# Experts one at a time with their weights as the moving operand, and a last stage in which ScalarE applies mean and deviation

## The reference

```
# mixture of experts, E = 64, rows gathered to 128 slots per expert
h  = silu(einsum('ecd,eid->eci', xb, w1)) * einsum('ecd,eid->eci', xb, w3)   # I = 176
yb = einsum('eci,edi->ecd', h, w2)                                           # D = 256
y  = zeros.at[tok].add(yb * weight)            # scattered back, added up
# second attention, after linear attention over 16 heads of 16
out = einsum('bhnd,bhde->bhne', qrh, kv) * z[..., None]
res = out + x
return (res - mean(res)) / sqrt(var(res) + 1e-12) * gamma + beta
# end of the model
x = x + s * silu(y + z)       # s: the attention's result
```

## Time and profile before

| | |
|---|---|
| median of 3 runs | 5537.14 us |
| the profiled execution | 5540.01 us, of which its span 5538.4 us |
| experts: first gather to last scatter | 5079.85 to 5310.77 us |
| last stage: from its first instructions to the end | 5316.9 to 5538.4 us |
| PE, DVE, ACT, POOL busy over the span | 89%, 75%, 54%, 53% |

### The profile page before, as it was taken

The page is one execution under the profiler, slowest core; times in us unless marked ns, Lnnn a source line. Parts: engine busy times, 40 slices in busy tenths (PEclk is TensorE's granted clock), DMA queues, the critical chain, the costliest instruction groups (busy, mean ns, idle before and its releaser), DMA issues. The chain is left out here.

```text
span 5538.4 us, 79645 instructions
## 1 busy us (share of the span) xinstructions
PE 4910.3 (89%) x26068; PEld 2909.0 (53%) x26068; DVE 4156.5 (75%) x8613; ACT 3011.0 (54%) x6489; POOL 2936.8 (53%) x1617
## 2 busy tenths in 40 slices
PE   6788888888885699999999999999999999998886
PEld 2233233233322477776555566666665555665765
DVE  3999999999999699999433477777763337995259
ACT  4877886887776477777211255555541114453232
POOL 4999999999999465655111244444431110002732
PEclk9898888889887799999999999999999999999997
DMA  5666566566555223223112111111111133444768
GB/s 134 152 157 148 142 160 159 139 150 160 147 132 129 77 85 91 86 88 103 46 57 63 45 35 35 37 38 36 46 52 47 57 117 129 159 141 126 196 147 177
DMA packets 493021, 585.39 MB, mean 106 GB/s; under 512 B 59446, under 2 KB 372548, under 8 KB 488516
## 3 DMA queue, kind: packets, MB, share of 16 engines
q1 hardware_dynamic: 461412, 554.19, 36.7%
q0 software_dynamic: 29184, 18.78, 2.3%
q10 hardware_dynamic: 2016, 7.34, 0.4%
HBM read 416.67 MB, written 180.37 MB: 108 GB/s over the span
## 5 line engine op out<-in xcount | busy, mean ns | idle before, releaser
L684 POOL TENSOR_TENSOR db<-durep,brep 128x2048 f32<-128x2048 f32 x256 | 1160.5, 4533 | 101.4 <-DVE p_h L589 87.6
L536 ACT ACTIVATE p_h<-dlrep,am 128x512 f32<-128x512 f32 x1024 | 700.4, 690 | 159.8 <-DVE hh L600 134.4
L589 DVE TENSOR_TENSOR_SCAN p_h<-p_h,hlast,db 128x512 f32<-128x512 f32 x576 | 718.3, 1278 | 21.8 <-ACT hlast L525 17.7
L1302 POOL TENSOR_TENSOR rot_cos<-rot_cos,rot_sin 128x1024 f32<-128x1024 f32 x128 | 302.2, 2361 | 536.1 <-DVE rot_sin L1223 536.1
L1298 POOL TENSOR_TENSOR rn<-n,mhalf 128x16 f32<-128x16 f32 x128 | 374.7, 2928 | 266.7 <-DVE n L1233 266.6
L600 DVE TENSOR_TENSOR hh<-p_h,crep 128x512 f32<-128x512 f32 x768 | 516.1, 672 | 0.0
L352 PE MATMUL p_acc<-hh,fold 128*32 128x512 f32 x2048 | 310.1, 681 | 207.4 <-DVE hh L600 206.1
L1665 POOL TENSOR_TENSOR grstd<-grstd,mhalf 128x4 f32<-128x4 f32 x32 | 32.6, 1019 | 729.1 <-DVE grstd L1582 728.9
L980 PE MATMUL p_s<-qkT 64*128 64x128 f32 x4096 | 300.3, 286 | 75.6 <-DVE nb L1188 74.4
L1567 ACT ACTIVATE gg<-p_s,b 128x512 f32<-128x512 f32 x160 | 110.0, 687 | 448.5 <-PE p_o L1510 265.8
L1091 ACT ACTIVATE probB<-probB,nb 128x256 f32<-128x256 f32 x512 | 254.4, 499 | 164.9 <-DVE nb L1188 164.9
(11 more groups left out here) (290 smaller groups left out, 11730.1 us busy)
## 6 DMA issues: line engine op xcount, KB each, us to landing
dlrep<-delta_rows SPq DMA_DIRECT2D x256, 256.0 KB
durep<-drive_rows SPq DMA_DIRECT2D x256, 256.0 KB
ew<-in_L_ffn_w SPq DMA_DIRECT2D x192, 176.0 KB
first_queries_keys<-qs SPq DMA_DIRECT2D x128, 256.0 KB, 2.4
qk<-first_queries_keys SPq DMA_DIRECT2D x64, 512.0 KB, 3.8
brep<-bc_rows SPq DMA_DIRECT2D x64, 256.0 KB
crep<-bc_rows SPq DMA_DIRECT2D x64, 256.0 KB
delta_rows<-dl SPq DMA_DIRECT2D x64, 256.0 KB
```

Of the source, the lines that this page charges most:

```text
L536: act.activation(p_h[:, (i % BANKS) * CH:(i % BANKS + 1) * CH], dlrep[use % 2][:, j], ACT.Exp, scale=am[:, q, j, g:g + 1]).then_inc(s_ex, 1)
L589: dve.tensor_tensor_scan(out=state, data0=bank, data1=db[s % 2][:, j], initial=0.0 if first else hlast[:, i % TILES:i % TILES + 1], op0=AL ...
L684: pool.tensor_tensor(out=db[s % 2][:], in0=durep[use % 2][:], in1=brep[c % 2][:, g:g + 1, :].to_broadcast([P, 4, CH]), op=ALU.mult).then_i ...
L1302: pool.tensor_tensor(out=rc[:], in0=rc[:], in1=rsn[:], op=ALU.add).then_inc(s_rot, 1)
```

## The change

In `experts`, the turned rows become the loaded operand and gate and up weights side by side (352 columns) the moving one. The result then has tokens on partitions, so before the down matmuls it must be turned: two transposes, and a copy by ScalarE (`ehT`). The experts no longer go in pairs: TensorE's loop pass `i` holds up of `i`, turning of the rows of `i + 2`, turning of the gated values of `i - 1`, and down of `i - 2`. GpSimd's and SyncE's programs in this block are the same.

In `final`, ScalarE applies mean and deviation (four activations of 128x256 with both as per-partition operands), VectorE then gamma and beta over the whole chunk (one instruction of 128x1024 each), and takes its moments ahead of the finish. GpSimd works out -mean·deviation in two more small instructions.

```diff
 # experts, TensorE
-            for m in range(0, NE, 2):
-                for e in (m, m + 1):            # turn both, then:
-                    for q, dst in ((0, p_g[a]), (1, p_u[a])):
-                        for b in range(2):
-                            for f in range(DH):
-                                ins = pe.matmul(dst[0:EB, b * P:(b + 1) * P], w13[k][:, f, q, b * EB:(b + 1) * EB],
-                                                xT[a][:, f, :], start=(f == 0), stop=(f == DH - 1))
+            def up(e):
+                pe.wait_ge(s_w[k], 48 * (e // U + 1))
+                if e > 1:
+                    pe.wait_ge(s_hd, e - 1)
+                pe.wait_ge(s_xT, e + 1)
+                for f in range(DH):
+                    ins = pe.matmul(p_gu[a][:, 0:2 * EI], xT[a][:, f, :], w13[k][:, f].rearrange("p q i -> p (q i)"),
+                                    start=(f == 0), stop=(f == DH - 1))
+            def turn_gated(e):
+                if e > 1:
+                    pe.wait_ge(s_hT, e - 1)
+                pe.wait_ge(s_hd, e + 1)
+                for b in range(2):
+                    ins = pe.transpose(p_h[a][0:EB, b * P:(b + 1) * P], hd[a][:, b * EB:(b + 1) * EB], ident[:])
+            def down(e):
+                if e > 1:
+                    pe.wait_ge(s_yb, e - 1)
+                pe.wait_ge(s_hT, e + 1)
+                for b in range(2):
+                    ins = pe.matmul(p_y[a][:, 0:D], hT[a][:, b, :], w2[k][:, b, :], start=(b == 0), stop=(b == 1))
+            turn_rows(0)
+            turn_rows(1)
+            for i in range(NE + 2):
+                if i < NE:
+                    up(i)
+                if i + 2 < NE:
+                    turn_rows(i + 2)
+                if 1 <= i <= NE:
+                    turn_gated(i - 1)
+                if i > 1:
+                    down(i - 2)
...
 # final, ScalarE
+            def normalise(c):
+                if c >= NB:
+                    act.wait_ge(s_out[c % NB], 16 * (c // NB))
+                act.wait_ge(s_nm, c + 1)
+                for j in range(CT):
+                    ins = act.activation(s1[c % NB][:, j], o[c % 2][:, j], ACT.Identity, bias=nm[c % 2][:, j:j + 1],
+                                         scale=rs[c % 2][:, j, 0:1])
+                ins.then_inc(s_nrm, 1)
...
                 if c + 1 < NC:
                     queries(c + 1)
+                if c > 0:
+                    normalise(c - 1)
                 gates(c)
+            normalise(NC - 1)
 # final, VectorE
             def finish(c):
-                dve.wait_ge(s_mv, c + 1)
-                for j in range(CT):
-                    ins = dve.scalar_tensor_tensor(out=s1[n][:, j], in0=o[k][:, j], scalar=mv[k][:, j, 0:1],
-                                                   in1=gam[:], op0=ALU.subtract, op1=ALU.mult)
-                ins.then_inc(s_ga, 1)
-                dve.wait_ge(s_ga, c + 1)
-                dve.wait_ge(s_rs, c + 1)
-                for j in range(CT):
-                    ins = dve.scalar_tensor_tensor(out=s1[n][:, j], in0=s1[n][:, j], scalar=rs[k][:, j, 0:1],
-                                                   in1=bet[:], op0=ALU.mult, op1=ALU.add)
-                ins.then_inc(s_be, 1)
+                dve.wait_ge(s_nrm, c + 1)
+                dve.tensor_tensor(out=s1[n][:], in0=s1[n][:], in1=gam[:].unsqueeze(1).to_broadcast([P, CT, D]),
+                                  op=ALU.mult).then_inc(s_ga, 1)
+                dve.wait_ge(s_ga, c + 1)
+                dve.tensor_tensor(out=s1[n][:], in0=s1[n][:], in1=bet[:].unsqueeze(1).to_broadcast([P, CT, D]),
+                                  op=ALU.add).then_inc(s_be, 1)
...
                 normaliser(c)
+                moments(c)
                 if c > 0:
                     finish(c - 1)
-                moments(c)
 # final, GpSimd: behind the power in power(c)
+                if c > 1:
+                    pool.wait_ge(s_nrm, c - 1)
+                pool.tensor_scalar(nm[c % 2][:], mv[c % 2][:, :, 0], -1.0, None, ALU.mult).then_inc(s_neg, 1)
+                pool.wait_ge(s_rs, c + 1)
+                pool.wait_ge(s_neg, c + 1)
+                pool.tensor_tensor(out=nm[c % 2][:], in0=nm[c % 2][:], in1=rs[c % 2][:].rearrange("p j a -> p (j a)"),
+                                   op=ALU.mult).then_inc(s_nm, 1)
```

More of the change, by code:

```diff
@@ new lines, in turn_rows @@
+            def turn_rows(e):
+                k, a = e % U, e % 2
+                if e > 1:
+                    pe.wait_ge(s_xT, e - 1)
+                pe.wait_ge(s_x[k], 16 * (e // U + 1))
+                for f in range(DH):
+                    ins = pe.transpose(p_t[a][:, f * P:(f + 1) * P], xe[:, k, f * P:(f + 1) * P], ident[:])
+                ins.then_inc(s_tr, 1)
+            def up(e):
+                k, a = e % U, e % 2
+                pe.wait_ge(s_w[k], 48 * (e // U + 1))
+                if e > 1:
+                    pe.wait_ge(s_hd, e - 1)
+                pe.wait_ge(s_xT, e + 1)
+                for f in range(DH):
+                    ins = pe.matmul(p_gu[a][:, 0:2 * EI], xT[a][:, f, :], w13[k][:, f].rearrange("p q i -> p (q i)"),
+                                    start=(f == 0), stop=(f == DH - 1))
+                ins.then_inc(s_up, 1)
@@ L2417, in _, with rows_turned @@
+            turn_rows(0)
[9 more added lines that the diff above has]
+                    down(i - 2)
         @block.scalar
         def _(act):
[L2419 to L2431, removed]
+            def rows_turned(e):
+                if e > 1:
+                    act.wait_ge(s_up, e - 1)
+                act.wait_ge(s_tr, e + 1)
+                act.activation(xT[e % 2][:].rearrange("p f t -> p (f t)"), p_t[e % 2][:, 0:D], ACT.Copy).then_inc(s_xT, 1)
@@ new lines, in silu, with gated_turned @@
+            def silu(e):
+                if e > 1:
+                    act.wait_ge(s_hd, e - 1)
+                act.wait_ge(s_up, e + 1)
+                act.activation(sg[e % 2][:], p_gu[e % 2][:, 0:EI], ACT.Silu).then_inc(s_sg, 1)
+            def gated_turned(e):
+                if e > 1:
+                    act.wait_ge(s_dn, e - 1)
+                act.wait_ge(s_trh, e + 1)
+                act.activation(hT[e % 2][:].rearrange("p b t -> p (b t)"), p_h[e % 2][0:EB, 0:2 * P],
+                               ACT.Copy).then_inc(s_hT, 1)
@@ L2433, in _ @@
+            rows_turned(0)
+            rows_turned(1)
+            for i in range(NE + 1):
+                if i < NE:
+                    silu(i)
+                if i + 2 < NE:
+                    rows_turned(i + 2)
+                if i > 0:
+                    gated_turned(i - 1)
         @block.vector
         def _(dve):
[L2435 to L2450, removed]
@@ new lines, in gate, with weigh @@
+            def gate(e):
+                a = e % 2
+                if e > 1:
+                    dve.wait_ge(s_trh, e - 1)
+                dve.wait_ge(s_sg, e + 1)
+                dve.tensor_tensor(out=hd[a][:], in0=p_gu[a][:, EI:2 * EI], in1=sg[a][:], op=ALU.mult).then_inc(s_hd, 1)
+            def weigh(e):
+                k, a = e % U, e % 2
+                if e >= U:
+                    dve.wait_ge(s_add[k], 16 * (e // U))
+                dve.wait_ge(s_x[k], 16 * (e // U + 1))
+                dve.wait_ge(s_dn, e + 1)
+                dve.tensor_scalar(yb[k][:], p_y[a][:, 0:D], xe[:, k, D + e:D + e + 1], None, ALU.mult).then_inc(s_yb, 1)
@@ L2452, in _ @@
+            for i in range(NE + 2):
+                if i < NE:
+                    gate(i)
+                if i > 1:
+                    weigh(i - 2)
         @block.gpsimd
@@ L2499, in final @@
     mv, rs = ([sb(f"{n}{k}", [P, CT, w]) for k in range(2)] for n, w in (("fmv", 2), ("frs", 1)))
+    nm = [sb(f"fnm{k}", [P, CT]) for k in range(2)]
+    s_neg, s_nm, s_nrm = (sem("f_" + n) for n in ("neg_mean", "nm", "normed"))
     p_q = [ps(f"fp_q{k}", CH) for k in range(4)]
@@ L2711, in normaliser @@
                 if c > 1:
-                    dve.wait_ge(s_ga, c - 1)
+                    dve.wait_ge(s_nrm, c - 1)
                 dve.wait_ge(s_rz, c + 1)
@@ L2732, in moments @@
                 if c > 1:
-                    dve.wait_ge(s_be, c - 1)
+                    dve.wait_ge(s_nm, c - 1)
                 for j in range(CT):
```

42 lines of the change are left out of this document (13 added, 29 removed).

## The result

| | before | changed |
|---|---|---|
| median, 12 runs each | 5539.73 us | 5555.26 us |
| lowest to highest | 5535.59 to 5542.24 | 5547.15 to 5559.42 |
| the profiled execution | 5540.01 | 5547.15 |
| its span | 5538.4 | 5545.5 |
| experts, first gather's start to last scatter's end | 230.9 | 220.9 |

The ratio is 1.0027 (95% interval 1.0019 to 1.0036): 15.5 us slower, where 5534 and no change were forecast. In the profiled executions the sum is -3.6 ahead of the experts (no code differs there) - 10.0 in the experts + 20.7 in the last stage = +7.1 us. The profiled execution of the changed kernel is the fastest of its twelve.

What follows compares the result with a forecast made beforehand. TensorE was taken to pace the experts (3.38 us each) and VectorE the last stage (11.96 per pass). Experts -6.5 and last stage +3.5 gave 5537.1 - 3.0 = 5534.1, forecast 5534 us, range 5521 to 5548.

Steps and rivals of the forecast that it cites:

- The loop is closed: Last stage: VectorE's next rotation waits for ScalarE, which waits for GpSimd and the pass's own variances; -0.05 us per pass.
- rival 2: Last stage: the loop isn't closed, VectorE's 11.16 us holds in twelve passes, the whole 5523; chance 0.20.
- Its length, 11.91 us: Last stage: the loop from one rotation's start to the next sums to 11.91 us, what a pass takes now.
- VectorE's own pass, 11.16 us: Last stage: a shorter finish saves VectorE 0.8 us per pass, so a pass could fall to 11.16.
- Second pass +2.5: Last stage, second pass, with the rotary tables' copy: next rotation at 5358.4 instead of 5355.85, +2.5 us.
- Last rotation to the end +1.5: Last stage: pass with the last rotation -0.8 us; at the end the unhidden way over GpSimd and ScalarE +2.3.
- Rival 4: Last stage: table loads cost more than their row; at double +31 us, the whole 5565; chance 0.04 in full.
- Experts -6.5: Experts: GpSimd sets 3.25 us per expert; -12.7 without stalls and +6.2 for late scatters give -6.5 us.
- Start: Experts: 1408 more columns ahead of the first down matmul, 1.2 us, so the first scatter at 5097.5.
- stalls: Experts: GpSimd waits for scatters that land late, which nothing hides any longer; +6.2 us.
- rival 1: Experts: the gather's loop sets the pace if rows take over 4.95 us; the whole about 5577; chance 0.07.
- Sum: Both blocks: experts -6.5 and last stage +3.5, together -3.0 us, no change that can be measured.

Runs made afterwards that it cites:

- e5: Changed kernel, but VectorE gives out a tile's variances right behind its moments, ahead of the finish of the tile before: 5524.47 us, ratio 0.9977.
- e1: Kernel before with only the experts' part of the change: 5534.18 us, ratio 0.9991.
- e3: Changed kernel with GpSimd's -mean made ahead of the power instead of behind it: 5540.81 us, ratio 1.0002.

## Why the prediction was wrong, by its steps

- *The loop is closed*: right. The activations stand ahead of the silu's table load in every pass, and rival 2 did not happen.
- *Its length, 11.91 us*: wrong, and this is the step that failed: "-mean and its product with the deviation 0.19 and 0.20 ... from the same kind of small instructions in the first stage". The product measured 1.18, held by VectorE's addition. The remaining terms (rotation to variances 3.18 for 3.13, power 1.04, activations 2.08 for 2.06, loads, silu and GELUs up to the rotation 5.04 for 4.98) are off by 0.18 in all: 11.91 + 0.98 + 0.18 = 13.07. A closed loop hands on every microsecond; the twelve passes (I had counted eleven) gave +11.4 where I had -0.5, nine of them +1.0 to +1.2, and the three with key sums, which took 13.0 before, +0.3, +0.1 and +1.1 (the product was held only in the last). I had taken durations from rows without asking what VectorE did beside them. The product of 0.20 at 147.84 in the earlier trace rows ran beside a scan that reads one operand from PSUM:

```profile
146.83 1.21 DVE L589 TENSOR_TENSOR_SCAN hs<-p_h,db 128x512 f32<-128x512 f32 x1
```

- *VectorE's own pass, 11.16 us*: 11.40 in `e5`, where nothing makes it wait. It decided nothing, but would have been 0.24 per pass too low.
- *Second pass +2.5*: +4.7. The added terms came out to the end of the tables' copy (11.33 us behind the rotation, as in the sum; the product wasn't held in this pass, 0.20). But TensorE, made to idle 4.93, came back at the lower clock, its matmuls took 2.36 more, and ScalarE's wait of 1.71 became 3.52. In `e5`, with the loop open, the pass takes 12.6, less than before.
- *Last rotation to the end +1.5* (-0.8 + 2.3): +4.6. From the last variances to the activations it is 3.3 us (5526.79 to 5530.11) where I had 1.7: the write's 1.35 ahead of the power had no term. Nor had the waits of 0.40 and 0.77 for ScalarE at the two finishes before.
- *Rival 4, table loads cost more*: it named 13 and more as its mark, and the passes are 13.07, but for another cause. A load starts 0.01 to 0.02 us behind the instruction before it in every row above, and lasts 1.28. The drain of about 1.38 us of which the Trainium skill speaks (ScalarE: Activation LUTs, What ACT_TABLE_LOAD costs) shows nowhere.
- *Experts -6.5*: -10.0 in the trace (5.3 over the runs of `e1`), GpSimd sets the pace as said. Start +1.0 (+1.2 said); 57 passes from 5093.80 to 5283.36 are 189.6, 57 x 3.25 and 4.3 of stalls (6.2 said); from there to the end 13.9 (15.2 said), because the last rows arrived within 2.5 us of their gather: started 5282.01, turned at 5284.50, and not 4.5. TensorE waits for `ex` as foreseen. The size of the stalls is near, their cause is not the one of the sum: of GpSimd's six waits of over 0.4 us in these passes one, of 1.29, ended with a scatter's landing, and five, that one among them, follow rows that came over 4.95 us behind their gather, the short bursts of rival 1.
- *Sum*: -10.0 + 20.7 = +10.7 in the two blocks, where I had -6.5 + 3.5. The sign was lost in one term, that of 0.2 us: without the hold (`e3`, which also takes the -mean off the path) the whole is 1.0002 of the kernel before. The second pass and the end, 5.2 us worse than said, are the rest of the miss.

## What to carry to other kernels

When a change makes a wait that closes a loop over several engines, price each short link by what runs beside it on the other engines, and not by its duration elsewhere: here 0.2 us became 1.2 and was paid in ten of the last twelve passes between rotations. Then look for the place from which the loop can be opened: giving out a result one step earlier (`e5`) turned 15.5 us lost into 12.9 gained, with every instruction the same. And a stage's end and its odd passes (another instruction in the queue, an engine that comes back slower) can cost nearly as much together as all the ordinary ones: 9.3 us here beside 11.4.

## What the runs showed of the hardware

- GpSimd's product of 128x4 in SBUF took 0.20 us beside VectorE's moments, 0.65 beside a 0.69 us multiplication of one operand, 1.18 beside a 1.23 us addition of two, and 1.07 beside the finish in `e5`. In all of them VectorE's instruction had started first and kept its own duration (the addition 1.23 with and without GpSimd beside it): GpSimd alone paid.
- After an idle of 4.93 us TensorE's eight rows of 128x512 took 6.03 us at a granted clock of 0.61, and 3.67 at 1.00 after idles of 0.45 and 1.32.
- TensorE's granted clock in the experts was 0.97 before and 0.96 after, at 198.0 and 173.8 us busy; with the gathers five ahead it was 0.86. In that kernel the same four rows of 352 columns take 2.55 us behind a wait of 3.63 and 1.35 elsewhere, a factor of 1.9, about that between the two levels of the clock (1.2 and 2.4 GHz):

```profile
5168.80 0.66 PE L2394 MATMUL ep_t<-ident,ex 128*128 128x128 f32 x2 [3.63 <-DMA ex<-rows_and_scores,take]
...
5171.39 2.55 PE L2404 MATMUL ep_gu<-ew,exT 128*128 128x352 f32 x4
...
5175.91 1.35 PE L2404 MATMUL ep_gu<-ew,exT 128*128 128x352 f32 x4
```
